# Score and maximum products of an attention kernel on halves of the array, two heads side by side

## Chip, cores and metric

One Trainium2 chip; the program runs on one of its cores. The metric is the time of one execution on the device, in microseconds. PE is the matmul engine (PEld its weight loads), DVE the vector engine, ACT the scalar engine, POOL the general one (GpSimd), SP the engine that issues most DMAs.

## What is computed

One transformer block on x of [4, 2048, 256] in fp32: causal attention with 16 heads of 16 dimensions, then a mixture of 16 experts (4 chosen per token) and one shared expert, each with its layer norm and modulation.

```python
h = layernorm(x) * (1 + ca) + sa
q, k, v = split(h @ qkv_w + qkv_b)             # [b, 16 heads, 2048, 16]
q, k = rotary(q), rotary(k)
scores = q @ k.T * 16 ** -0.5                  # causal mask
x = x + ga * ((softmax(scores) @ v) @ out_w + out_b)
h = layernorm(x) * (1 + cb) + sb
tidx, tw = route(h)                            # 4 of 16 experts
x = x + gb * (sum_e combine_e * w2_e(silu(w1_e h) * (w3_e h)) + shared(h))
```

## The kernel before

`plan()` writes one list of work items by hand; each engine walks the list in the same order and issues its part of each item, with semaphore waits between engines. So the list alone sets the order on all engines and on the queues of SP and POOL.

**qkv stage.** 16 chunks of 512 tokens. Rotated q and k are split into three bf16 parts each (high, middle, low: k = 0, 1, 2), stored to memory as `qk_parts`. The maxima of head group 0 are computed in between (`early`, `fill`), in PSUM banks 1 and 7 in turn.

**Attention.** A group is four heads of one batch; 16 groups (g), each with 40 steps (i) of 128 keys by up to 512 queries. Parts are loaded into `QO` and `KO` (three sets, in turn) by items `loadg`, 9 loads a group (L719), laid out along the partitions so that one product of 96 rows adds up six part products: q0k0, q1k0, q2k0, q0k1, q1k1, q0k2. Two more rows, 96 and 97, hold the negated row maximum in two bf16 parts on the query side (POOL's DMA, L1599) and ones on the key side.

- `max` (L930 to L933): for the group to come, queries in 128 rows against up to 512 keys; on the diagonal a second product (identb by m1, 128 rows) adds the mask. DVE reduces each bank (L1334), 160 a group. The banks are 4, 5 and 6 in turn (`Units`); a product waits until the reduction of three before it is done. `neg` and `nturn` (L939, L1347, L1349) turn the maxima of one head into a row.
- `st` (L952): four scores a step, 98 rows, one head each, into banks 0 to 3; `exp` (ACT, L1502) takes two banks at a time. POOL cuts the diagonal (L1619).
- `pv` (L971): four value products in fp32, each on its own 32 columns of the array, two steps behind.
- projection, norm and router logits of a finished batch (`project`, L983, L993, L1004), routing of the first half (`route`, on DVE) and its scatter (`scatter`, POOL's indirect DMAs, L1669) are pumped in, so many slots a step.

Between the four scores of a step stand single maxima: st, max, st, exp, max, pv, max, st, max, st, exp.

**Expert stage.** 143 + 143 jobs of 128 slots and 64 jobs of the shared expert, a pipeline of four items (`jin` L1022, `jgate` L1033, `jturn` L1046, `jdown` L1060). In the first 143 jobs the rest of the last batch's projection, the routing of the second half and its scatter are pumped at 2.65 slots a job: one list, one rate. SP loads the rows to scatter (L801), the rows of the jobs (L819), and stores the results (L833), all in one queue.

## Time and profile before

| | |
|---|---|
| runs | 3535.3, 3529.62, 3533.96 us; median 3533.96 |
| profiled execution | 3538.17 us, its span 3536.4 us |
| granted PE clock, mean | 0.949 |
| busy PE / DVE / ACT / POOL | 3129.2 / 2286.6 / 1608.0 / 1313.5 us |
| attention, first to last exponential | 347.7 to 2326.4 us |
| head groups 1, 2, 5, 6 | 106.8 us each |
| groups with projection (3, 4, 7, 8, 11, 12) | 128 to 143 us |
| groups 9, 10, 13, 14, 15 | 120.0, 117.3, 139.3, 119.4, 92.7 us |
| expert stage | from 2328 us to the end |

A group ends with its fourth copy of the outputs (L1509). A record of PE shows the time until the result is modelled to be there, so records overlap; how long PE is held is read from one start to the next.

### The profile page before, as it was taken

How to read it: one execution, taken by the hardware profiler on the slowest of the kernel's cores; microseconds unless marked ns; L12 is line 12 of the kernel's file. 1: busy time of each engine (PE TensorE's matmuls, PEld its weight loads, DVE VectorE, ACT ScalarE, POOL GpSimd, SP SyncE). 2: the span in 40 equal slices, each digit the busy share in tenths (PEclk: the TensorE clock that was granted, in tenths of full speed). 3: DMA queues.
4: the chain of work that ended last, by engine and by line, in shares of the span. 5: the costliest groups of instructions: out<-in, count | busy, mean ns of one | idle time of the engine just before them, and what ended most of it. 6: DMA issues, size and time to landing. Idle time of an engine off the chain costs nothing.

```text
span 3536.4 us, 50303 instructions
## 1 busy us (share of the span) xinstructions
PE 3129.2 (88%) x17106; PEld 1518.3 (43%) x17108; DVE 2286.6 (65%) x4981; ACT 1608.0 (45%) x2593; POOL 1313.5 (37%) x1684
## 2 busy tenths in 40 slices
PE   8776799999999999999998888989986779999778
PEld 4433233344333344233343222346654446666555
DVE  8887588887788877999877767224631124443466
ACT  3322466655566654566554555733322223333222
POOL 6755111234212244211265555331025543331453
PEclk9998899999999999999999989989997889999899
DMA  5733521232122213212234432343344445553565
GB/s 171 196 94 109 89 51 31 46 79 71 39 56 51 54 52 79 47 29 47 62 109 105 104 90 77 116 111 95 96 130 148 152 136 148 146 148 114 151 181 154
DMA packets 280103, 350.21 MB, mean 99 GB/s; under 512 B 58968, under 2 KB 236776, under 8 KB 279592
## 3 DMA queue, kind: packets, MB, share of 16 engines
q1 hardware_dynamic: 248972, 271.79, 29.5%
q0 software_dynamic: 30208, 71.87, 6.9%
q10 hardware_dynamic: 672, 3.34, 0.4%
q8 instruction: 141, 2.31, 0.3%
q14 instruction: 110, 0.90, 0.1%
HBM read 206.51 MB, written 139.21 MB: 98 GB/s over the span
## 4 chain that ended last, share of the span: by engine, by line
PE 67%; DVE 16%; issue 6%; another core or an unknown queue 4%; DMA 2%; POOL 2%; ACT 2%; SPq 1%; DVEq 0%; POOLq 0%; ACTq 0%
PE PB L930 13%; PE PB L1033 13%; PE PB L971 12%; DVE mx L1334 10%; PE PB L952 9%; PE PB L1060 8%; PE PB L983 3%; PE PB L1046 2%; PE PB L1022 2%; PE PB L933 1%; PE PB L901 1%; DMA KO<-qk_parts 1%; DVE xn L1287 1%; PE PB L912 1%
## 5 line engine op out<-in xcount | busy, mean ns | idle before, releaser
L1334 DVE TENSOR_REDUCE mx<-PB 128x1 f32<-128x512 f32 (+3 forms) x2560 | 1409.0, 602 | 289.5 <-PE PB L933 149.3
L1502 ACT ACTIVATE P<-PB 128x1024 f32<-128x1024 f32 (+3 forms) x1280 | 1102.3, 895 | 812.7 <-PE PB L952 759.1
L930 PE MATMUL PB<-KO,QO 96*128 96x512 bf16 (+3 forms) x2560 | 901.0, 357 | 105.9 <-DVE mx L1334 67.8
L952 PE MATMUL PB<-QO,KO 98*128 98x512 bf16 (+3 forms) x2560 | 824.2, 353 | 16.0 <-DVE PB L1359 11.6
L971 PE MATMUL PB<-P,V 128*17 128x512 f32 (+3 forms) x5120 | 605.3, 545 | 17.0 <-POOL P L1619 16.7
L930 PEld LDWEIGHTS PB<-KO,QO 96*128 96x128 bf16 x2560 | 251.0, 98 | 789.7 <-DVE mx L1334 517.4
L1033 PE MATMUL PB<-W,xT 128*128 (+1 forms) x1400 | 554.3, 521 | 40.0 <-issue 32.7
L1426 DVE TENSOR_TENSOR ha<-sl,PB 128x192 f32<-128x192 f32 x350 | 123.7, 353 | 535.4 <-ACT sl L1547 406.7
L1060 PE MATMUL PB<-W,haT 96*128 (+1 forms) x1400 | 381.6, 396 | 62.1 <-issue 34.0
L1619 POOL TENSOR_SCALAR_AFFINE_SELECT P<-P 128x256 f32<-128x256 f32 x512 | 207.4, 414 | 582.7 <-ACT P L1502 578.0
L1682 POOL DMA_INDIRECT yg<-y_slots,sidu x256 | 244.0, 953 | 396.4 <-DVE acc L1418 191.9
L952 PEld LDWEIGHTS PB<-QO,KO 98*128 98x128 bf16 x2560 | 243.6, 100 | 247.2 <-ACT P L1502 91.5
L1033 PEld LDWEIGHTS PB<-W,xT 128*128 128x128 f32 x1400 | 253.9, 202 | 160.0 <-issue 75.1
L1554 ACT ACTIVATE haT<-PB 96x256 f32<-96x256 f32 x350 | 132.7, 379 | 388.2 <-PE PB L1046 259.5
L1547 ACT ACTIVATE sl<-PB 128x192 f32<-128x192 f32 x350 | 115.5, 330 | 403.6 <-PE PB L1033 281.7
L1060 PEld LDWEIGHTS PB<-W,haT 96*128 96x128 f32 x1400 | 248.2, 197 | 94.4 <-issue 57.4
L933 PE MATMUL PB<-m,identb 128*128 128x128 bf16 x1024 | 229.4, 224 | 0.0
L1669 POOL DMA_INDIRECT x_slots<-Rsg,sidu x172 | 166.8, 970 | 89.3 <-issue 44.4
L1434 DVE COPY yo<-PB 128x256 f32<-128x256 f32 x286 | 120.6, 422 | 115.7 <-PE PB L1060 49.9
L1046 PE MATMUL PB<-ident,ha 128*96 128x128 f32 x700 | 142.2, 285 | 57.0 <-DVE ha L1426 38.7
L1599 POOL DMA_DIRECT2D QO<-nh x128 | 66.7, 523 | 307.6 <-DVE nh L1349 305.8
L971 PEld LDWEIGHTS PB<-P,V 128*17 128x17 f32 x5120 | 85.8, 95 | 201.1 <-issue 165.0
(157 smaller groups left out, 2821.8 us busy)
## 6 DMA issues: line engine op xcount, KB each, us to landing
xq<-x_slots SPq DMA_DIRECT2D x286, 128.0 KB
y_slots<-yo SPq DMA_DIRECT2D x286, 128.0 KB
qk_parts<-pt SPq DMA_DIRECT2D x192, 128.0 KB, 2.4
KO<-qk_parts SPq DMA_DIRECT2D x96, 256.0 KB, 5.3
rden<-rden_rows SPq DMA_DIRECT2D x256, 64.0 KB
QO<-qk_parts SPq DMA_DIRECT2D x16, 768.0 KB, 7.9
v_rows<-vst SPq DMA_DIRECT2D x16, 544.0 KB, 3.4
V<-v_rows SPq DMA_DIRECT2D x16, 544.0 KB, 5.9
```

What stands on the lines that cost most here:

```text
L930: mm = pe.matmul(PB[:, bank, 0:n], QO[0:96, k3, j, 128 * t:128 * t + 128], KO[0:96, k3, j, 512 * kc:512 * kc + n], start=True, stop=True)
L933: mm = pe.matmul(PB[:, bank, n - 128:n], identb[:, :], m1[:, :], start=False, stop=True, skip_group_check=True)
L952: mm = pe.matmul(PB[:, j, 0:n], KO[0:98, k3, j, 128 * kt:128 * kt + 128], QO[0:98, k3, j, q0:q0 + n], start=True, stop=True)
L971: mm = pe.matmul(PB[32 * j:32 * j + 17, 7, c0:512], V[:, g % 2, kt, 17 * j:17 * j + 17], P[:, pbuf(g, i, j // 2), j % 2, 0:n], start=kt == ...
L1033: mm = pe.matmul(PB[:, 2 + k, 0:2 * I], xT[:, k, f, :], W13[f][:, expert(n), :], start=f == 0, stop=f == 1)
L1046: mm = pe.transpose(PB[0:IH, 4 + k, 128 * f:128 * f + 128], ha[:, k, IH * f:IH * f + IH], ident[:, :])
L1060: mm = pe.matmul(PB[:, bank, 0:256], haT[:, k, f, :], W2[f][:, expert(n), :], start=f == 0, stop=f == 1)
L1334: dve.tensor_reduce(mx[:, j, t, kc:kc + 1], PB[:, u.bank[item], 0:n], AX.X, ALU.max).then_inc(s["mx"], 1)
L1502: act.activation(P[:, pbuf(g, i, p), :, 0:n], PB[:, 2 * p:2 * p + 2, 0:n], ACT.Exp, scale=0.25).then_inc(s["exp"], 1)
L1619: pool.affine_select(out=P[:, k, :, 0:128], in_=P[:, k, :, 0:128], compare_op=ALU.is_ge, fill=0.0, base=0, pattern=[[0, 2], [1, 128]], cha ...
L1669: pool.indirect_dma_start(xg_d[p][:, :], bass.IndirectOffsetOnAxis(sidu[:, i, j:j + 1], 0), hs[k], None).then_inc(s[f"w_s{p}{k}"], 16)
L1682: pool.indirect_dma_start(yg[:, k, j, :], None, y_d[p][:, :], bass.IndirectOffsetOnAxis(sidu[:, i, j:j + 1], 0)).then_inc(s[f"l_yg{k}"], 16)
```

## The change

- **Layout.** Each head uses 98 of 128 partitions in two parts. For an even head of the group, rows 0 to 63 hold four part products (q0k0, q1k0, q0k1, q1k1), rows 64 to 95 the other two (q2k0, q0k2), rows 96 and 97 the maximum. For an odd head the halves are swapped: 64 to 127, 0 to 31, 32 and 33. The loads are 20 a group (`LOADS`), each for two heads, one a step instead of one every third step.
- **Maxima.** A product of 64 rows over four part products. `max_items` gives the heads of a pair in turn, so neighbours stand in different halves of the array; their `neg` and `nturn` come after both. The mask is two products of 64 rows, of 128 and 64 columns (`pick`, `tri`).
- **Scores.** `st` issues two heads' first passes (64 rows) side by side; `st2` waits for both (semaphore `sa`) and adds two second passes (34 rows) in the other half of the array, into the same banks. Maxima stand between `st` and `st2`.
- **Pumps in the first 143 jobs.** Projection and routing at 4 slots a job; the scatter, once the routing is done, at 1.8.
- `tile_e0` and `tile_e1` share one tile, at partitions 0 and 32.

```diff
+LOADS = [(z, 64 * odd + row, odd, k, n) for odd in (0, 1)
+         for z, row, k, n in ((0, 0, 0, 2), (0, 32, 0, 2), (1, 0, 0, 1), (1, 16, 0, 1), (1, 32, 1, 1), (1, 48, 1, 1))]
+LOADS += [(z, 64 - 64 * odd + row, odd, k, 1) for odd in (0, 1) for z, row, k in ((0, 0, 2), (0, 16, 0), (1, 0, 0), (1, 16, 2))]
+NL = len(LOADS)
...
-    for j in range(4):
+    for j in (0, 2):
         for t in range(16):
             for kc in range(t // 4 + 1):
                 yield ("max", g, j, t, kc)
-        yield ("neg", g, j)
-        yield ("nturn", g, j)
+                yield ("max", g, j + 1, t, kc)
+        for k in (j, j + 1):
+            yield ("neg", g, k)
+            yield ("nturn", g, k)
...
             o("st", g, i, 0)
-            one()
-            o("st", g, i, 1)
+            maxima((done + want + 2) // 4 * 2)
+            o("st2", g, i, 0)
             o("exp", g, i, 0)
-            one()
             if len(pend) == 2:
                 values(*pend.pop(0))
-            one()
-            o("st", g, i, 2)
-            one()
-            o("st", g, i, 3)
+            o("st", g, i, 1)
+            maxima(want)
+            o("st2", g, i, 1)
             o("exp", g, i, 1)
...
-            if g < 14 and 0 <= part < 27 and part % 3 == 0:
-                o("loadg", g + 2, part // 3)
+            if g < 14 and 0 <= part < NL:
+                o("loadg", g + 2, part)
...
-    run(0, NI[0], (chain(proj[3], route(1), scatter(1)), 2.65))
+    run(0, NI[0], (chain(proj[3], route(1)), 4), (chain(once("route", 1, ROUTE_SLOTS - 1), scatter(1)), 1.8))
...
-                    mm = pe.matmul(PB[:, bank, 0:n], QO[0:96, k3, j, 128 * t:128 * t + 128], KO[0:96, k3, j, 512 * kc:512 * kc + n],
+                    half = slice(64 * (j % 2), 64 * (j % 2) + 64)
+                    mm = pe.matmul(PB[:, bank, 0:n], QO[half, k3, j, 128 * t:128 * t + 128], KO[half, k3, j, 512 * kc:512 * kc + n],
                                    start=True, stop=True)
                     if kc == t // 4:
-                        mm = pe.matmul(PB[:, bank, n - 128:n], identb[:, :], m1[:, :], start=False, stop=True, skip_group_check=True)
+                        pe.matmul(PB[:, bank, n - 128:n], pick[half, 0, :], tri[half, 0, :], start=False, stop=True, skip_group_check=True)
+                        mm = pe.matmul(PB[:, bank, n - 64:n], pick[half, 1, :], tri[half, 1, 64:128], start=False, stop=True,
+                                       skip_group_check=True)
...
+                    for j in (2 * p, 2 * p + 1):
+                        rows = slice(64 * (j % 2), 64 * (j % 2) + 64)
+                        pe.matmul(PB[:, j, 0:n], KO[rows, k3, j, 128 * kt:128 * kt + 128], QO[rows, k3, j, q0:q0 + n],
+                                  start=True, stop=False).then_inc(s["sa"], 1)
+                elif name == "st2":
...
+                    q.wait_ge(s["sa"], 2 * o.n(*item))
+                    for j in (2 * p, 2 * p + 1):
+                        rows = slice(64 - 64 * (j % 2), 98 - 64 * (j % 2))
+                        mm = pe.matmul(PB[:, j, 0:n], KO[rows, k3, j, 128 * kt:128 * kt + 128], QO[rows, k3, j, q0:q0 + n],
+                                       start=False, stop=True)
+                    mm.then_inc(s["st"], 1)
```

**Where it moves instructions.** The order on PE in group 5, between the value products of steps 19 and 20 (counted from 0), before (maxima L930, mask L933, scores L952, values L971):

```order
L930 MATMUL PB<-KO,QO 128x512
L933 MATMUL PB<-m_51,identb 128x128
L952 MATMUL PB<-QO,KO 128x384
L930 MATMUL PB<-KO,QO 128x512
L952 MATMUL PB<-QO,KO 128x384
L930 MATMUL PB<-KO,QO 128x512
L952 MATMUL PB<-QO,KO 128x256
L930 MATMUL PB<-KO,QO 128x128
L933 MATMUL PB<-m_51,identb 128x128
L952 MATMUL PB<-QO,KO 128x256
L930 MATMUL PB<-KO,QO 128x512
L971 MATMUL PB<-P,V 17x512 x4
```

The same place in the changed kernel (maxima L941, masks L944 and L945, first passes L968, second passes L979, values L997):

```order
L968 MATMUL PB<-QO,KO 128x384 x2
L941 MATMUL PB<-KO,QO 128x512 x2
L979 MATMUL PB<-QO,KO 128x384 x2
L968 MATMUL PB<-QO,KO 128x256 x2
L941 MATMUL PB<-KO,QO 128x256
L944 MATMUL PB<-tri,pick 128x128
L945 MATMUL PB<-tri,pick 128x64
L941 MATMUL PB<-KO,QO 128x256
L944 MATMUL PB<-tri,pick 128x128
L945 MATMUL PB<-tri,pick 128x64
L979 MATMUL PB<-QO,KO 128x256 x2
L997 MATMUL PB<-P,V 17x512 x4
```

Scores come in pairs with maxima between the passes. Over all groups 1060 of 1280 second passes have a maximum ahead of them since their first pass; the 220 others are 22 in group 0, 80 in group 15, and 118 in the rest. Diagonal maxima of a pair stand three products apart.

The order on PE in the qkv stage (qk L901, v L912 and group 0's maxima), before:

```order
L901 MATMUL PB<-hT,wqk_s 128x512
L930 MATMUL PB<-KO,QO 128x128
L933 MATMUL PB<-m_51,identb 128x128
L901 MATMUL PB<-hT,wqk_s 128x512
L930 MATMUL PB<-KO,QO 128x256
L933 MATMUL PB<-m_51,identb 128x128
```

and changed (qk L911, v L922):

```order
L911 MATMUL PB<-hT,wqk_s 128x512
L941 MATMUL PB<-KO,QO 128x256
L944 MATMUL PB<-tri,pick 128x128
L945 MATMUL PB<-tri,pick 128x64
L911 MATMUL PB<-hT,wqk_s 128x512
L941 MATMUL PB<-KO,QO 128x512 x2
L922 MATMUL PB<-wv_s,hT 128x256 x2
```

The fp32 products of the qkv stage and the bf16 products alternate as before. What differs is that the bf16 ones now take halves of the array: passing from an undivided product to one in row halves or back occurs 184 times here and 353 times in attention, where before both used the whole array.

The order on SP in the expert stage while POOL scatters (L801 loads rows for the scatter), before:

```order
L801 DMA Rsg<-h_rows 128x256
L833 DMA y_slots<-yo 128x256
L819 DMA xq_146<-x_slots 128x256
L801 DMA Rrk<-h_rows 128x256
L833 DMA y_slots<-yo 128x256
L819 DMA xq_146<-x_slots 128x256
L833 DMA y_slots<-yo 128x256
L819 DMA xq<-x_slots 128x256
L801 DMA Rsg<-h_rows 128x256
L833 DMA y_slots<-yo 128x256
```

and changed (L811 is the same load, L843 the store, L829 the jobs' load):

```order
L811 DMA Rrk<-h_rows 128x256
L843 DMA y_slots<-yo 128x256
L829 DMA xq<-x_slots 128x256
L843 DMA y_slots<-yo 128x256
L829 DMA xq<-x_slots 128x256
L811 DMA Rsg<-h_rows 128x256
L843 DMA y_slots<-yo 128x256
L829 DMA xq<-x_slots 128x256
L843 DMA y_slots<-yo 128x256
L829 DMA xq_145<-x_slots 128x256
L843 DMA y_slots<-yo 128x256
```

A load for the scatter stands after every one or two jobs before, after every two or three in the changed kernel; the scatter goes from job 56 to 136 instead of from 86 to 140.

## Rows read from the trace of the kernel before

**Rows 1.** Busy time by stretch: groups 1, 9, 13 and 15 of attention, whole engines.

```profile
core 0: us, PE busy (x) PEld busy (x) DVE busy (x) ACT busy (x) POOL busy (x), PEclk, DMA share, GB/s
494.90:601.70 106.80, 104.33 (x710) 36.43 (x708) 90.56 (x177) 69.56 (x86) 21.78 (x44) 1.00 0.24 47
...
1459.00:1579.00 120.00, 109.77 (x710) 35.72 (x708) 111.41 (x230) 70.12 (x86) 24.39 (x44) 0.99 0.21 41
...
1976.40:2115.80 139.40, 116.84 (x709) 37.61 (x708) 92.77 (x177) 70.85 (x86) 84.23 (x109) 0.89 0.42 111
...
2235.20:2327.90 92.70, 87.71 (x576) 32.85 (x576) 12.20 (x45) 69.14 (x89) 40.32 (x69) 1.00 0.39 124
```

**Rows 2.** Groups of instructions by shape in group 1: busy, mean ns, idle before.

```profile
L1334 DVE TENSOR_REDUCE mx<-PB 128x1 f32<-128x512 f32 x113 | 72.2, 682 | 5.9 <-PE PB L930 4.1 <-PE PB L933 0.9
...
L930 PE MATMUL PB<-KO,QO 96*128 96x512 bf16 x113 | 42.9, 382 | 0.5 <-DVE mx L1334 0.4
...
L971 PE MATMUL PB<-P,V 128*17 128x512 f32 x224 | 29.5, 598 | 0.0
```

**Rows 3.** Timeline of group 5: start us, us, engine line op, in order of time.

```profile
1001.50 0.38 PE L952 MATMUL PB<-QO,KO 98*128 98x512 bf16 x1
...
1001.92 1.02 ACT L1502 ACTIVATE P<-PB 128x1024 f32<-128x1024 f32 x1 [0.55 <-PE PB L952]
...
1006.38 0.38 PE L930 MATMUL PB<-KO,QO 96*128 96x512 bf16 x1
...
1006.69 1.05 PE L971 MATMUL PB<-P,V 128*17 128x512 f32 x8
...
1007.68 0.39 PE L930 MATMUL PB<-KO,QO 96*128 96x512 bf16 x1
...
1007.90 0.38 PE L952 MATMUL PB<-QO,KO 98*128 98x512 bf16 x1
...
1008.12 0.38 PE L930 MATMUL PB<-KO,QO 96*128 96x512 bf16 x1
...
1008.34 0.22 PE L933 MATMUL PB<-m,identb 128*128 128x128 bf16 x1
...
1008.40 0.38 PE L952 MATMUL PB<-QO,KO 98*128 98x512 bf16 x1
```

**Rows 4.** Timeline of DVE in group 10: reductions without a wait.

```profile
1590.13 2.47 DVE L1334 TENSOR_REDUCE mx<-PB 128x1 f32<-128x512 f32 x4
```

**Rows 5.** Waits in group 1: engine line <- waited for: us in total, times, longest.

```profile
PEld PB L930 <- DVE mx L1334: 29.9, 56, 0.9
```

**Rows 6.** Waits in group 15.

```profile
PEld PB L952 <- ACT P L1502: 29.2, 42, 0.9
```

**Rows 7.** Timeline of group 15: score products followed by a projection.

```profile
2265.80 0.60 PE L952 MATMUL PB<-QO,KO 98*128 98x512 bf16 x2
...
2266.24 1.89 PE L983 MATMUL PB<-wo_s,ON 128*128 128x256 f32 x8
```

**Rows 8.** Waits in the second half of the qkv stage.

```profile
PEld PB L930 <- DVE mx L1334: 55.8, 75, 3.8
```

**Rows 9.** SP's queue and PE's wait at the start of attention.

```profile
364.21 1.39 SPq L719 DMA_DIRECT2D QO<-qk_parts  x3
365.65 3.22 SPq L719 DMA_DIRECT2D KO<-qk_parts  x6
...
PEld PB L930 <- DMA KO<-qk_parts: 21.9, 1, 21.9
```

**Rows 10.** Expert stage by stretch: L1060 alone, then L1022 alone.

```profile
2450.00:2500.00 50.00, 19.11 (x74) 12.21 (x72) 1.00 0.32 95
...
3000.00:3100.00 100.00, 37.65 (x147) 25.11 (x148) 1.00 0.50 145
...
2613.00:2880.00 267.00, 23.89 (x112) 17.82 (x112) 0.83 0.46 149
```

**Rows 11.** Waits of SP's queue, ACT and POOL in time, while scatters run.

```profile
SPq L833 <- DVE yo L1434: 118.4, 27, 12.9
...
2712.43 0.38 ACT L1554 ACTIVATE haT<-PB 96x256 f32<-96x256 f32 x1 [6.73 <-remote]
...
2708.00 0.96 POOL L1669 DMA_INDIRECT x_slots<-Rrk,sidu  x1 [0.30 <-issue]
2709.27 0.96 POOL L1669 DMA_INDIRECT x_slots<-Rrk,sidu  x1 [0.30 <-issue]
```

More of the change, by code:

```diff
@@ L182, in plan @@
         if c == 5:
-            for part in range(9):
+            for part in range(NL):
                 o("loadg", 0, part)
@@ L268, in plan @@
     proj = [project(b) for b in range(4)]
-    for part in range(9):
+    for part in range(NL):
         o("loadg", 1, part)
@@ L370, in run, with once @@
             drain(f[0])
-    run(0, NI[0], (chain(proj[3], route(1), scatter(1)), 2.65))
+    def once(name, *at):
+        while not o.has(name, *at):
+            yield
+    run(0, NI[0], (chain(proj[3], route(1)), 4), (chain(once("route", 1, ROUTE_SLOTS - 1), scatter(1)), 1.8))
     o("second")
@@ L857, in expert @@
                     half = i // RB % 2 * RB
-                    pe.load(pe_regs[half:half + k], tile_e[p][0:1, i:i + k])
+                    pe.load(pe_regs[half:half + k], tile_e[p][:, i:i + k])
                     for j in range(k):
```

77 lines of the change are left out of this document (43 added, 34 removed).

## Prediction

> **What bounds the kernel now.** I read the busy time of each stretch first, because the profile's 88% for PE is an average over stages with different limits. Attention runs 16 head groups of 40 steps. A group without projection work, such as group 1, takes 106.8 us; there PE is busy 104.3 us, DVE 90.6 and ACT 69.6 [rows 1]. In group 9 the routing joins and DVE reaches 111.4 of 120.0. In group 13 POOL scatters. Group 15 has no maxima left, and DVE falls to 12.2 of 92.7. Next the groups of instructions inside group 1: DVE stood idle only 5.9 us before the 113 widest reductions, PE 0.5 us before the widest maxima [rows 2]. So both are near their limits, and PE is the tighter one.
>
> PE's records are longer than what they occupy, so I read starts. In group 5 a 512-column bf16 product is followed by the next start after 0.22 us, though its record says 0.38; a 128-column one after 0.06 [rows 3]. The value product (L971, eight records side by side) starts 0.31 us after the product ahead of it, 0.09 more than 0.22, and holds the array 0.99 us, where four streams of 0.22 would need 0.86: 0.13 more. The mean product is 435 columns wide (24 full steps and 16 averaging 320), 0.185 us. Group 1 then needs 320 products x 0.185 = 59.2, 64 masks x 0.06 = 3.8, 40 value products x (0.09 + 0.13 + 0.74) = 38.4, in all 101.4 us of its 106.8; the rest is mostly four turns of the maxima, before which PE waits for DVE. DVE needs 0.60 us for a 512-column reduction: four take 2.47 us, of which the last record is 0.68 [rows 4]. An off-diagonal maximum therefore gives PE 0.22 plus its share of the step's other work, (59.2/2 + 38.4)/160 = 0.43, together 0.65, against DVE's 0.60. That is the parity which limits what a faster PE can bring.
>
> **The maxima.** Each head now contracts 64 rows in its own half of the array, and two heads stand side by side. Off the diagonal there are 96 products in a group (24 per head), 48 pairs; if the halves overlap, a pair costs 0.22 instead of 0.44, so 48 x 0.22 = -10.6 us per group. No row shows two row halves at once. The nearest is L971: eight records with a mean of 598 ns lie in 0.99 us [rows 2, 3], four column strips side by side. Bounds: no overlap, 0 gained; full overlap, -10.6. I take full overlap, since L971 is the same array divided the other way. On the diagonal the order puts three products of one head before three of the other, so only the last 64 columns meet the partner: no gain there. The split mask is a second instruction, 0 to 0.06 us; 64 x 0.04 = +2.6 us.
>
> **The scores.** Four products a step become eight, in four pairs. With overlap the streaming is equal; four steps of 128 columns gain 4 x 4 x 0.056 = +0.9 us, because they are issue-bound. Without overlap it would be 160 x 0.185 = +29.6 us per group. The second pass waits for the semaphore of the first. A record of 0.38 us against a start distance of 0.22 leaves 0.16 us, and about 0.04 for the signal (ACT starts 0.04 us after such a record's end, 1001.92 against 1001.88), 0.2 us in all [rows 3]. What covers it is one pair of maxima (0.22). The order has 1060 of 1280 second passes with at least one maximum ahead. The 118 without that lie outside group 15 and group 0's start are 8 a group x 0.2 = +1.6; those with a single narrow one +0.6; the weight load that is no longer fetched early, 80 x 0.02 (bounds 0 and 0.10, its record) = +1.6. Behind that wait on PE stand the second pass, the value product and the next maxima; ACT's exponential waits for the second pass, and DVE, when it catches up, for the maxima.
>
> Per group: -10.6 + 2.6 + 0.9 + 1.6 + 0.6 + 1.6 = -3.3 us. DVE's floor of about 90 us allows it, but a pair needs two of three banks free at once. PE already waited 29.9 us before weight loads of maxima for DVE in group 1 [rows 5], mostly hidden under the product ahead. I keep -3.3 in groups 1 to 7 (-23) and half in groups 8 to 14 (-12), where DVE or the scatters end more waits. Groups 0 (11 steps) and 15 (40) have no maxima: 102 waits x 0.2 = +20, of which I take +14, because PE waits 29.2 us for ACT in group 15 anyway and may hide some [rows 6]. Maxima and scores together: **-21 us**.
>
> **Changes of the array's division.** Before, maxima, scores, projection, turns and qkv all used the undivided array, and PE passed between them without a gap: two score products start at 2265.80 and the projection 0.44 us later, just 2 x 0.22 [rows 7]. Only the value product divides it, and pays 0.09 going in and 0.13 coming out. Now every bf16 product is in row halves, so each meeting with an undivided fp32 product is a new change: counted from the order, 353 in attention and 184 in the qkv stage. Bounds: 0 (the 0.22 belongs to L971's column strips or to fp32 alone) and 0.11 each, 39 + 20 = +59 us. I take **+24 us**, under half: in the qkv stage PE waits for DVE before the maxima as it is (55.8 us over 75 waits [rows 8]), which covers some. The Trainium skill (TensorEngine Tiling (Array Packing), Key Properties) says that changing the tiling mode drains the engine. By that rule all 537 changes would cost; the trace agrees with it for the value product [rows 3], and no run here shows it for row halves.
>
> **Loads and small work.** A group's parts come in 20 loads instead of 9, with the same bytes; from group 2 on one a step, a group ahead of their readers, where SP has time. One place is exposed: group 1's loads are issued in a burst, from 364.21 on, nine in 4.6 us, and PE then waits 21.9 us for them before the first maximum [rows 9]. Twenty issues at 0.5 us put the last one 5.5 us later. Bounds: 0 (bytes decide) and +5.5; I take **+3 us**. The same burst for group 0 lies in the qkv stage beside other work, and behind it SP's stores of parts have time to spare: 0, with +5.5 if they have not. POOL's rows of negated maxima keep number and size; the DVE setup instructions added lie ahead of the first chunk, about 1 us.
>
> **The expert stage.** The pumps are changed too. The last projection and routing go at 4 slots a job, the scatter at 1.8 instead of 2.65. In the order the scatter began at job 86 and ended at 140; now it runs from 56 to 136. Before it a job (four L1060 records, 18.4 jobs in 50 us) takes 2.7 us; during it two L1022 records a job make 56 jobs in 267 us, 4.8 each [rows 10]. SP waits 118.4 us there for DVE's output copies, not for the scatters, and ACT once sits 6.73 us before work that is ready, put down to "remote" [rows 11]. So the scatters slow 54 jobs by 2.1 us each, 113 us, or 0.8 us per POOL instruction (145). If that price is per scatter, thinning them brings nothing: 0. If the scatters' time is their own (255 us for 145, whatever the jobs do), 80 jobs fit where 54 did: 26 x 2.7 = -70 us. The gathers later, one per job of 2.7 us, show no such price, which speaks for one that falls with density. I take **-25 us**, nearer the first end, because 1.8 times POOL's spacing of 1.26 us [rows 11] is still 2.27 of a 2.7 us job. That case would be wrong on the other side if every job during scatters is slowed: 26 more jobs at up to 2.1 us, +55.
>
> **Sum.** -21 + 24 + 3 - 25 = -19 us on the profiled execution's 3538.17: 3519. The median of the runs shown is 3533.96, 4 us lower, so **3515 us**, 0.5% below it. About 0.2%, 7 us, is what can be told from no change.
>
> **Rivals.**
> 1. *The changes of division are dear*: PE empties the array at all 537. The rule of the Trainium skill named above (TensorEngine Tiling (Array Packing), Key Properties) would have it so. The sum is -21 + 59 + 3 - 25 = +16, 3534 + 16 = 3550 us, slower. It decides from 43 us on, 0.08 us each, if the tail gives 25. For: the 0.22 us around every L971. Against: PE has slack in the qkv stage. Chance 0.22.
> 2. *The halves overlap badly.* With half the overlap, scores cost +15 and maxima save 5 less: +17 us in each of 15 groups, 3534 + 255 = 3790; with none, 29.6 x 16 over 4000. Against: L971's strips. For: no row shows row halves. Chance 0.08.
> 3. *Better than forecast.* PE's relief pays in full, -7 a group to DVE's floor (-100), the tail gives -60, and changes of division cost nothing: 3534 - 100 + 14 - 60 = 3390; half of it, 3450, is more likely. Chance 0.22.
> 4. *DVE keeps the pace*: bursts of two maxima into three banks leave it as late as before, attention gains nothing and the scatters keep their price: 3534 + 14, then 0 to 24 more: 3548 to 3572. Chance 0.13.
>
> My forecast keeps 0.35, spread over 3495 to 3540. Cases 1, 2 and 4 and a part of mine are slower: 0.38; within 0.2%: 0.14; faster: 0.48. The range reaches to 3430 (case 3 in part) and 3610 (case 1 with case 4), leaving out case 2 and the far end of case 3.
>
> **What would show it.** Right: two maxima of neighbouring heads start within 0.06 us, and a pair is followed after 0.22; second passes start about 0.43 us after the first; group 1 takes 103 to 105 us; group 15 100 to 107; scatter jobs fall from 4.7 us to about 4. A gap of 0.1 us before a projection that follows a score shows case 1. Pairs 0.4 us apart show case 2. Group 1 unchanged with DVE idle under 5 us shows case 4. The forecast is wrong if attention, from 347.7 to 2327.9 before, changes by over 60 us either way.

## The result, and the profile after

Four executions of the changed kernel took 3696.03 to 3703.71 us, median 3701.64; four of the kernel before on the same chip 3529.62 to 3535.3, median 3534.32. The ratio is 1.0475, 95% interval 1.0458 to 1.0491: slower by 4.7%. The forecast was 3515 us, range 3430 to 3610. It was wrong in sign and out of its range.

The profiled execution of the changed kernel has a span of 3702.0 us, 165.6 more than before. I cut both spans at the same places (a group ends with its fourth copy of the outputs):

| stretch, us | before | after | difference | forecast |
|---|---|---|---|---|
| up to the first exponential (qkv stage) | 347.7 | 358.2 | +10.5 | part of +24 |
| group 0 | 147.2 | 162.4 | +15.2 | about +3, and loads +3 |
| groups 1, 2, 5, 6 | 106.8 each | 115.8 each | +9.0 each | -3.3 each |
| groups 3, 4, 7 | 128.5, 137.2, 128.5 | 140.0, 144.8, 139.9 | +30.5 | -9.9 and part of +24 |
| groups 8 to 14 | 919.0 | 1008.2 | +89.2 | -12 and part of +24 |
| group 15 | 92.7 | 111.1 | +18.4 | about +11 |
| the rest (expert stage) | 1208.6 | 1174.2 | -34.4 | -25 |

The busy time by stretch in the changed kernel, for groups 0, 1, 9, 13 and 15 in this order; the last four answer to [rows 1]:

```profile
358.20:520.60 162.40, 135.86 (x969) 37.93 (x967) 92.42 (x183) 75.07 (x86) 21.43 (x45) 0.83 0.35 65
520.60:636.40 115.80, 106.84 (x935) 33.14 (x934) 89.84 (x177) 72.29 (x85) 21.84 (x44) 1.00 0.20 43
...
1562.60:1695.00 132.40, 119.11 (x934) 35.42 (x934) 111.01 (x230) 72.94 (x85) 23.86 (x44) 0.91 0.18 38
...
2127.40:2286.90 159.50, 119.74 (x933) 34.72 (x932) 90.95 (x177) 72.93 (x85) 82.77 (x106) 0.87 0.34 96
2416.70:2527.80 111.10, 103.84 (x731) 35.40 (x732) 12.19 (x45) 69.94 (x88) 40.34 (x69) 1.00 0.32 105
```

In group 1 the clock is fully granted, DVE works as long as before (89.84 against 90.56), and both engines idle more: DVE 26.0 us instead of 16.2. No engine got a new amount of work that fills the 9 us; most of it is waiting. The groups of instructions by shape in group 1, which answer to [rows 2]:

```profile
L1365 DVE TENSOR_REDUCE mx<-PB 128x1 f32<-128x512 f32 x113 | 71.0, 683 | 15.3 <-PE PB L941 14.2 <-PE PB L945 1.0
...
L941 PE MATMUL PB<-KO,QO 64*128 64x512 bf16 x113 | 31.9, 379 | 3.9 <-DVE mx L1365 2.3
```

DVE stood idle 15.3 us before the widest reductions, 5.9 before the change: it now waits for PE's maxima. And PE's waits in the same group, beside [rows 5]:

```profile
PEld PB L941 <- DVE mx L1365: 20.2, 48, 0.7
...
DVE mx L1365 <- PE PB L941: 14.2, 24, 1.0
...
DVE mx L1365 <- PE PB L945: 8.3, 8, 3.8
PEld PB L979 <- PE PB L968: 9.0, 29, 0.4
```

So PE and DVE wait for each other in turn, and PE waits for itself (the second pass for the first). The sum of the weight loads' waits for DVE is no measure of the loss: it was 29.9 us before and is 20.2 now, and much of it lies under products that still run. The timeline of PE's products in group 5 shows how; columns are start us, us, engine, line and operation:

```profile
1067.55 0.39 PE L968 MATMUL PB<-QO,KO 64*128 64x512 bf16 x2
1067.77 0.38 PE L941 MATMUL PB<-KO,QO 64*128 64x512 bf16 x2
1068.03 0.39 PE L979 MATMUL PB<-QO,KO 34*128 34x512 bf16 x2
1068.25 0.38 PE L968 MATMUL PB<-QO,KO 64*128 64x512 bf16 x2
1068.47 0.84 PE L941 MATMUL PB<-KO,QO 64*128 64x512 bf16 x2
1068.94 0.60 PE L979 MATMUL PB<-QO,KO 34*128 34x512 bf16 x2
```

The halves do overlap. Two products of 512 columns stand in one record of 0.39 us, and the next pair starts 0.22 us later: each pair costs what one product did. But the second pair of maxima (1068.47) finds one bank free where it needs two, and its second product waits for DVE. DVE and PE's weight loads at the same place:

```profile
1068.18 1.89 DVE L1365 TENSOR_REDUCE mx<-PB 128x1 f32<-128x512 f32 x3 [0.72 <-PE PB L941]
...
1068.93 0.09 PEld L941 LDWEIGHTS PB<-KO,QO 64*128 64x128 bf16 x1 [0.58 <-DVE mx L1365]
```

DVE had idled 0.72 us until the first pair came (1068.18). 0.29 us later the second pair begins, and its second product waits until 1068.93. Two pairs, 0.7 us apart, want four banks and there are three; then value products pass in which DVE gets nothing new. No run gave the maxima a fourth bank.

The second loss is plain in group 15, which has no maxima. Its timeline, beside [rows 7]:

```profile
2480.28 0.39 PE L979 MATMUL PB<-QO,KO 34*128 34x512 bf16 x2
2480.60 0.62 PE L1030 MATMUL PB<-gw_s,lT 128*128 128x16 f32 x4
2481.07 0.41 PE L1019 MATMUL PB<-ident,h2t 128*128 128x128 f32 x2
2481.42 0.39 PE L968 MATMUL PB<-QO,KO 64*128 64x512 bf16 x2
2481.90 0.39 PE L979 MATMUL PB<-QO,KO 34*128 34x512 bf16 x2
2482.22 1.05 PE L997 MATMUL PB<-P,V 128*17 128x512 f32 x8
2483.20 0.39 PE L968 MATMUL PB<-QO,KO 64*128 64x512 bf16 x2
2483.68 0.39 PE L979 MATMUL PB<-QO,KO 34*128 34x512 bf16 x2
```

The second passes start 0.48 us after the first (2483.20, 2483.68), where the 512 columns would allow 0.22: 0.26 uncovered, twice a step, 80 times in the group, an estimate of 20.8 us. The waits of group 15 put it down by name; the second line answers to [rows 6]:

```profile
PEld PB L979 <- PE PB L968: 29.9, 77, 0.6
PEld PB L968 <- ACT P L1533: 18.6, 26, 0.9
```

The third loss is in the same timeline: from a pair in halves to an undivided product it takes 0.32 us (2480.28, 2480.60), not 0.22.

A fourth part of the loss stands in the clock column of the rows. TensorE's clock was granted at one of two levels, 2.4 or 1.2 GHz, and a mean below 1.00 stands for time at the lower one, which counts as one half. Group 0 has 0.83; before, the same group had 0.90:

```profile
347.70:494.90 147.20, 119.59 (x728) 35.91 (x727) 92.12 (x182) 74.41 (x87) 21.46 (x45) 0.90 0.41 71
```

Group 9 has 0.91 and had 0.99 [rows 1]. From PE's timeline in group 9, with the clock at its lower level from about 1639.0 to 1649.2:

```profile
1636.85 0.85 PE L941 MATMUL PB<-KO,QO 64*128 64x512 bf16 x2 [1.09 <-DVE mx L1365]
...
1647.34 1.91 PE L997 MATMUL PB<-P,V 128*17 128x512 f32 x8
1649.18 0.41 PE L968 MATMUL PB<-QO,KO 64*128 64x512 bf16 x2
```

PE had waited 1.09 us for DVE shortly before the clock fell, and the value product then holds the array 1.84 us instead of 0.98 (2482.22 to 2483.20). What a stretch loses to the clock is therefore at most its length times what its mean lacks of 1.00. By this estimate group 0 lost 27.6 us against 14.7 before, group 9 11.9 against 1.2, and the whole span 3702.0 x 0.063 = 233 against 3536.4 x 0.051 = 180. So up to some 53 of the 165.6 us are time at the lower clock: 8 of the +10.5 in the qkv stage, 13 of the +15.2 in group 0, about 48 of the +89.2 in groups 8 to 14, about 5 in groups 3, 4 and 7, none in groups 1, 2, 5, 6 and 15; and about 20 of the 34.4 us that the expert stage gained. Whether PE's new waits brought the lower clock or only stand beside it, no run here parts.

### The profile page after: what moved, and what is told of

Same layout as the page of the kernel before. It is cut to its first block, busy times and chain, and to the rows that moved or that the text cites. A ratio compares the mean times of both kernels' runs of the same rounds, so it can differ in the third digit from the quotient of the medians.

```text
span 3702.0 us, 57660 instructions
## 1 busy us (share of the span) xinstructions
PE 3237.6 (87%) x20690; PEld 1482.0 (40%) x20692; DVE 2273.4 (61%) x4990; ACT 1638.6 (44%) x2593; POOL 1314.9 (36%) x1685
## 4 chain that ended last, share of the span: by engine, by line
PE 40%; DVE 9%; another core or an unknown queue 5%; issue 3%; ACT 1%; POOL 1%; DMA 1%; SPq 0%; DVEq 0%; POOLq 0%; ACTq 0%
PE PB L1059 12%; PE PB L1086 7%; DVE mx L1365 6%; PE PB L997 6%; PE PB L968 3%; PE PB L941 3%; PE PB L979 3%; PE PB L1072 2%; PE PB L1048 2%; PE PB L1009 2%; ACT sl L1578 0%; ACT P L1533 0%; PE PB L1030 0%; ACT xT L1569 0%
## 5 line engine op out<-in xcount | busy, mean ns | idle before, releaser
L1533 ACT ACTIVATE P<-PB 128x1024 f32<-128x1024 f32 (+3 forms) x1280 | 1135.0, 896 | 967.9 <-PE PB L979 908.8
L941 PE MATMUL PB<-KO,QO 64*128 64x512 bf16 (+3 forms) x2560 | 684.3, 360 | 146.3 <-DVE mx L1365 99.2
L979 PE MATMUL PB<-QO,KO 34*128 34x512 bf16 (+3 forms) x2560 | 598.6, 366 | 53.6 <-remote 35.6
L997 PE MATMUL PB<-P,V 128*17 128x512 f32 (+3 forms) x5120 | 624.9, 561 | 4.0 <-POOL P L1652 3.9
L968 PE MATMUL PB<-QO,KO 64*128 64x512 bf16 (+3 forms) x2560 | 498.4, 366 | 13.6 <-DVE PB L1390 12.1
L941 PEld LDWEIGHTS PB<-KO,QO 64*128 64x128 bf16 x2560 | 198.4, 96 | 478.2 <-DVE mx L1365 372.6
L968 PEld LDWEIGHTS PB<-QO,KO 64*128 64x128 bf16 x2560 | 137.7, 95 | 552.2 <-issue 287.9
L1578 ACT ACTIVATE sl<-PB 128x192 f32<-128x192 f32 x350 | 115.5, 330 | 378.7 <-PE PB L1059 269.6
L979 PEld LDWEIGHTS PB<-QO,KO 34*128 34x128 bf16 x2560 | 154.4, 94 | 228.7 <-PE PB L968 172.6
L1702 POOL DMA_INDIRECT x_slots<-Rsg,sidu x172 | 166.6, 968 | 138.2 <-DMA Rsg<-h_rows 94.6
L1661 POOL TENSOR_TENSOR ON<-osb,rden 128x512 f32<-128x512 f32 x64 | 82.5, 1289 | 352.7 <-DMA rden<-rden_rows 266.5
L944 PE MATMUL PB<-tri,pick 64*128 64x128 bf16 x1024 | 193.5, 223 | 0.0
```

The lines of the kernel that those rows point to most:

```text
L941: mm = pe.matmul(PB[:, bank, 0:n], QO[half, k3, j, 128 * t:128 * t + 128], KO[half, k3, j, 512 * kc:512 * kc + n], start=True, stop=True)
L944: pe.matmul(PB[:, bank, n - 128:n], pick[half, 0, :], tri[half, 0, :], start=False, stop=True, skip_group_check=True)
L968: pe.matmul(PB[:, j, 0:n], KO[rows, k3, j, 128 * kt:128 * kt + 128], QO[rows, k3, j, q0:q0 + n], start=True, stop=False).then_inc(s["sa"], 1)
L979: mm = pe.matmul(PB[:, j, 0:n], KO[rows, k3, j, 128 * kt:128 * kt + 128], QO[rows, k3, j, q0:q0 + n], start=False, stop=True)
L997: mm = pe.matmul(PB[32 * j:32 * j + 17, 7, c0:512], V[:, g % 2, kt, 17 * j:17 * j + 17], P[:, pbuf(g, i, j // 2), j % 2, 0:n], start=kt == ...
L1533: act.activation(P[:, pbuf(g, i, p), :, 0:n], PB[:, 2 * p:2 * p + 2, 0:n], ACT.Exp, scale=0.25).then_inc(s["exp"], 1)
```

## The experiments

The chips differ. On one the kernel before took about 3357 us (e1 to e6), on the others 3526 to 3543. The same kernel was profiled on a quick chip and on a slow one as e1 and e15: groups 12 to 14 and the expert stage, in which POOL scatters or gathers, hold the whole difference (1408.7 and 1585.5 us), and group 1 takes 106.8 us on both, as the changed kernel's takes 115.8 wherever it was profiled. So times are compared as ratios to the kernel before on the same chip, and groups by their own length.

### The pumps, alone and undone

`e1` is the kernel before with the new pumps, `e2` the changed kernel with the old ones.

```diff
-    run(0, NI[0], (chain(proj[3], route(1), scatter(1)), 2.65))
+    run(0, NI[0], (chain(proj[3], route(1)), 4), (chain(once("route", 1, ROUTE_SLOTS - 1), scatter(1)), 1.8))
```

> The kernel before with the changed pumps alone: projection and routing at 4 slots a job, the scatter at 1.8. Theory A (thinned scatters slow the jobs less, whatever attention does): the expert stage, 1209 us before and 1174 in the changed kernel, takes 1174, so 3500 us. Rival (the stage gained only because of what attention left it with): 3534 us.

> The changed kernel with the pumps of before (one list at 2.65). Theory A: the expert stage goes back to 1209 us, 3702 + 35 = 3737 us, attention as it was. Rival: 3702 us.

Measured: e1 3339.1 us, ratio 0.9948 (0.9931 to 0.9964); e2 3532.19 us, 1.0521 (1.0503 to 1.0539). The pumps gain 19 us on this chip; what is slower is all in the halves. On the chip of the first result the stretch after attention shrank by 34.4 us, and the windows show where. Columns here are those of [rows 10]; the scatters' stretch of before, then of after (PE's L1022 and L1048, two records a job):

```profile
2646.60:2866.00 219.40, 20.07 (x92) 14.85 (x92) 0.82 0.46 149
```

```profile
2776.80:3023.00 246.20, 28.67 (x144) 21.41 (x144) 0.92 0.50 161
```

46 jobs at 4.77 us became 72 at 3.42, with 128 scatters in either stretch. The price of a job does fall with the scatters' density. Part of the fall is the clock's (0.82 and 0.92): without at most 0.86 and 0.27 us a job, by the estimate above, 3.91 and 3.15 are left.

### Bursts and the wait of the second pass

`e4` issues the maxima one at a time again, one between the passes of each pair of heads, one on either side of the value product, and what is left at the step's end:

```diff
-            maxima((done + want + 2) // 4 * 2)
+            one()
             o("st2", g, i, 0)
             o("exp", g, i, 0)
+            one()
             if len(pend) == 2:
                 values(*pend.pop(0))
+            one()
             o("st", g, i, 1)
-            maxima(want)
+            one()
             o("st2", g, i, 1)
             o("exp", g, i, 1)
+            while done < want:
+                one()
```

> The changed kernel with its maxima placed one at a time (one between the passes, one on either side of the value product, one between the passes) in place of two bursts. Theory B (bursts of two into three banks leave holes of 1.7 us in which DVE runs dry, then PE waits for banks): group 1 falls from 115.8 us to 108 to 110, 3702 - 80 = 3620 us. Theory C (what costs is the wait of the second pass, which one maximum covers about as well as two, and pairs that no longer stand together add up to 10.6 us a group): group 1 stays or grows, 3702 to 3800 us.

`e5` lets the second pass read rows of the half in which the first ran, and so needs no wait. It leaves two part products and the row maximum out, and it moves the pass to the other half as it drops the wait; no run parts these two, and "the wait" below stands for both:

```diff
-                    q.wait_ge(s["sa"], 2 * o.n(*item))
...
-                        rows = slice(64 - 64 * (j % 2), 98 - 64 * (j % 2))
+                        rows = slice(64 * (j % 2), 64 * (j % 2) + 34)
```

> The changed kernel with the second pass in the same half of the array as the first and so with no wait between them; it adds 34 rows of the first half in place of the two part products and the maximum, so the scores are others. Group 15 has a second pass 0.48 us behind the first, 0.22 of it streaming: 80 x 0.26 = 21 us. Theory C: group 15 falls from 111 to 92 us and group 1 by 6 us or more, 3702 - 110 = 3590 us. Theory B: group 15 falls as much, but group 1 by 2 us at most, 3702 - 50 = 3650 us.

`e7` is both, and `e9` the changed kernel once more, beside it. All of e3, e4, e5 and e7 hold the new pumps, so a ratio below 1 is not the halves' gain by itself.

> Spread maxima (as in the run before) and the second pass in the same half without a wait (it adds 34 rows of the first half, so the scores are others). Group 1 was 115.8 with bursts, 115.1 with bursts and no wait, 110.0 spread. If the wait costs only where nothing covers it: group 1 at 108.5 to 110, group 15 at 94.7. If the bursts hid the wait's price: group 1 at 106.8 or below.

> The changed kernel once more, beside the kernel before on the chip of these runs. The kernel with the old pumps was at 3532 us beside 3358, and the pumps alone took 19 us off the kernel before: so 3515 us, a ratio of 1.047 as in the first comparison. Group 1 at 115.8 us.

| | ratio (interval) | group 1 | group 15 |
|---|---|---|---|
| changed kernel (e9) | 1.0476 (1.0448 to 1.0504) | 115.8 | 111.0 |
| e4, no bursts | 1.0297 (1.0266 to 1.0328) | 110.0 | 111.1 |
| e5, no wait | 1.0366 (1.0349 to 1.0383) | 115.1 | 94.7 |
| e7, neither | 0.9942 (0.9919 to 0.9964) | 103.1 | 95.4 |

In group 1 the wait alone is worth 0.7 us and the bursts alone 5.8, but both together 12.7: while one is there, it stands in for much of the other. All of group 1's rows have a clock of 1.00, so none of this is the clock's. Group 15 splits them: without maxima only the wait counts, 16.4 us of its +18.4. In e4, with the bursts gone, the wait for the first pass comes forward; its row in group 1, where the changed kernel has 9.0:

```profile
PEld PB L983 <- PE PB L972: 22.9, 64, 0.6
```

The same spacing takes group 0 from 162.4 to 147.6 us with all 20 loads left as they are, so its +15.2 came with the bursts and not with the loads. Its clock rose with it, from 0.83 to 0.86, which is up to 7 of the 14.8 us.

### Whether the pairs pay

`e3` takes the heads' maxima in turn again, so that no two neighbours are in different halves:

```diff
-    for j in (0, 2):
+    for j in range(4):
         for t in range(16):
             for kc in range(t // 4 + 1):
                 yield ("max", g, j, t, kc)
-                yield ("max", g, j + 1, t, kc)
...
+        yield ("neg", g, j)
+        yield ("nturn", g, j)
```

> The changed kernel with the maxima of one head after the other, as before, so neighbours stand in the same half and cannot overlap each other. If overlap is worth what the forecast took, PE loses up to 10.6 us a group: group 1 from 115.8 to 122 to 126 us, 3702 + 110 = 3810 us. If the overlap is hidden under waits for DVE and for the second pass: group 1 within 2 us, 3702 +- 30 us.

Measured: 3538.0 us, 1.0534 (1.0505 to 1.0563), against 1.0521 (1.0503 to 1.0539) for e2 and 1.0476 (1.0448 to 1.0504) for the whole change on another chip. Group 1 takes 116.1 us against 115.8. The overlap of the maxima, forecast at 10.6 us a group, is worth 0.3 in this order; what the whole program shows of it lies in groups 0 (176.6 us, 163.9 in e2) and 8 (161.2, 150.5), and there the clock fell from 0.83 to 0.76 and from 0.92 to 0.86, by the estimate 15 and 11 us, as much as the difference. `e10` (changed) and `e11` (before) ask whether DVE hides it: DVE reduces half the columns only.

```diff
-                    dve.tensor_reduce(mx[:, j, t, kc:kc + 1], PB[:, u.bank[item], 0:n], AX.X, ALU.max).then_inc(s["mx"], 1)
+                    dve.tensor_reduce(mx[:, j, t, kc:kc + 1], PB[:, u.bank[item], 0:n // 2], AX.X, ALU.max).then_inc(s["mx"], 1)
```

> The changed kernel with DVE reducing only the first half of each tile of scores (it leaves the other half out of the maxima). Theory B (PE has room, the pace of DVE through three banks takes it back): group 1 falls from 115.8 us to 102 or less, below the 106.8 of the kernel before, since PE's need was put at 103.5. If PE itself is the longer one now: group 1 stays above 110 us.

> The kernel before with the same halved reductions. PE's need there was worked out at 101.4 us and the turns: group 1 falls from 106.8 to 102 to 104 us. If DVE held it as much as it holds the changed kernel: below 98 us.

Measured: e10 3477.98 us, 0.9837 (0.9811 to 0.9863), group 1 102.8 us; e11 3411.17 us, 0.9648 (0.9611 to 0.9685), group 1 103.8. The busy time of group 1 in e10, then in e11 (DVE's busy time stands behind PE's and PEld's):

```profile
479.40:582.20 102.80, 100.90 (x935) 32.92 (x934) 55.01 (x176) 70.76 (x86) 21.88 (x44) 1.00 0.23 49
```

```profile
459.40:563.20 103.80, 102.76 (x709) 36.53 (x708) 63.29 (x177) 69.48 (x86) 21.77 (x44) 1.00 0.26 48
```

With DVE out of the way the changed order needs 1.0 us less of PE than the old one, and with DVE at work 9.0 more: waits on DVE cost it 13.0 us and the kernel before 3.0. These 10.0 more and 1.0 less are the +9.0.

### The changes of division

`e6` is the kernel before with maxima of 64 rows, two of six part products left out, in one half of the array, beside masks, scores and projection of 96 to 128 rows. In group 1 the array's division then changes 336 times instead of 80, by the order of instructions.

```diff
-                    mm = pe.matmul(PB[:, bank, 0:n], QO[0:96, k3, j, 128 * t:128 * t + 128], KO[0:96, k3, j, 512 * kc:512 * kc + n],
+                    mm = pe.matmul(PB[:, bank, 0:n], QO[0:64, k3, j, 128 * t:128 * t + 128], KO[0:64, k3, j, 512 * kc:512 * kc + n],
```

> The kernel before with its maxima over rows 0 to 63 in place of 0 to 95 (it leaves two of the six part products out of the maxima), everything else and the order unchanged: undivided scores and masks alternate with products in a row half. Theory D (each change of the array's division costs 0.1 us, as the gaps of 0.09 and 0.10 around a projection in the changed kernel show): about ten changes a step more, 40 us a group on PE's path, group 1 from 106.8 to 140 us, 3534 + 500 = 4030 us. Rival (a product of 64 rows is no change by itself, the gaps come from the fp32 type): 3534 us.

Measured: 3833.38 us, 1.1426 (1.1361 to 1.149); group 1 130.1 us. 23.3 us more over 256 changes are 0.091 each (0.103 if e11's 103.8 is taken for PE's need before), and the timeline of PE in group 1 shows them one by one:

```profile
603.12 0.23 PE L933 MATMUL PB<-m,identb 128*128 128x128 bf16 x1
603.19 0.38 PE L952 MATMUL PB<-QO,KO 98*128 98x512 bf16 x1
603.50 0.39 PE L930 MATMUL PB<-KO,QO 64*128 64x512 bf16 x1
603.82 0.23 PE L933 MATMUL PB<-m,identb 128*128 128x128 bf16 x1
603.89 0.38 PE L952 MATMUL PB<-QO,KO 98*128 98x512 bf16 x1
```

From 603.19 to 603.50 is 0.31 us for 512 columns (undivided to half), from 603.50 to 603.82 is 0.32 (half to undivided), where 0.22 passes without a change; mask to score, both undivided, takes 0.07 (603.12, 603.19), against 0.06 in the kernel before [rows 3].

### The value product between the passes

`e8` gives the second pass of the second pair another cover, e4's value product, which takes 1 us:

```diff
+            o("st", g, i, 1)
             one()
             if len(pend) == 2:
                 values(*pend.pop(0))
             one()
-            o("st", g, i, 1)
-            one()
             o("st2", g, i, 1)
             o("exp", g, i, 1)
+            one()
```

> Spread maxima, and the value product moved between the two passes of the second pair, so that it covers one of a step's two waits. In group 15, where nothing else covers them, 40 of 80 waits of 0.26 us go: 111.1 to 101 us; in group 1, where single maxima covered most of a wait, 110.0 to 108.5. Whole 3457 - 35 = 3422 us beside a kernel before of 3357. If ACT's later exponential holds the banks instead: no gain, 3457 us.

Measured: 3694.09 us, 1.0473 (1.0443 to 1.0502), group 1 117.6 us against e4's 110.0, and group 15, for which 101 was expected, 115.5 against 111.1 (at most 3.5 of it at a lower clock, 0.97). A miss. In group 1 the wait for the first pass shrank as meant, but PE now waits for ACT to free the scores' banks (18.8 us, 3.4 in e4) and for DVE (34.6, 27.8 in e4). In group 15 the waits for the first pass even grew, from 29.6 us in e4 to 43.9. PE's weight loads in group 1:

```profile
PEld PB L945 <- DVE mx L1369: 34.6, 57, 0.9
PEld PB L972 <- ACT P L1537: 18.8, 34, 0.8
...
PEld PB L983 <- PE PB L972: 5.5, 14, 0.9
```

The first pass of the second pair now stands ahead of the value product, earlier than ACT has read its banks; the wait was moved in group 1, not covered. Why it grew in group 15 stays open.

### Both passes in a head's own half

`e12` keeps all part products and needs no wait: the second pass's operands of a head lie in that head's half, in the tile's column of its neighbour (`j ^ 1`); the two heads of a pair swap the places of these operands. The loads' column and POOL's rows of negated maxima move with them. On e4:

```diff
-LOADS += [(z, 64 - 64 * odd + row, odd, k, 1) for odd in (0, 1) for z, row, k in ((0, 0, 2), (0, 16, 0), (1, 0, 0), (1, 16, 2))]
+LOADS += [(z, 64 * odd + row, odd, k, 1) for odd in (0, 1) for z, row, k in ((0, 0, 2), (0, 16, 0), (1, 0, 0), (1, 16, 2))]
...
-                    q.wait_ge(s["sa"], 2 * o.n(*item))
...
-                        rows = slice(64 - 64 * (j % 2), 98 - 64 * (j % 2))
-                        mm = pe.matmul(PB[:, j, 0:n], KO[rows, k3, j, 128 * kt:128 * kt + 128], QO[rows, k3, j, q0:q0 + n],
+                        rows, sl2 = slice(64 * (j % 2), 64 * (j % 2) + 34), j ^ 1
+                        mm = pe.matmul(PB[:, j, 0:n], KO[rows, k3, sl2, 128 * kt:128 * kt + 128], QO[rows, k3, sl2, q0:q0 + n],
```

> Spread maxima, and each head's second pass in its own half: its two part products and its maximum rows lie in the neighbour's column slot of the same half, so all six part products and the maximum are there and no wait stands between the passes. Theory E (burst and wait each cost only where the other does not hide it; without both PE keeps a small gain): group 1 at 103.1 us as in the run that left parts out, group 15 at 95, ratio 0.994 to the kernel before. Rival (that run was quicker for another reason, its operands or loads): group 1 above 108 us, ratio 1.02.

`e13` is e12 with two maxima at a time again, one pair ahead of the value product and one behind it; `e14` is e12 with half the columns reduced (the edit of e10). The diff is that of e13.

```diff
-            one()
...
-            one()
+            upto = (done + want + 2) // 4 * 2
+            while done < min(upto, want):
+                one()
...
-            one()
+            while done < (want if want == len(mu) else want // 2 * 2):
+                one()
...
-            one()
...
-            while done < want:
-                one()
```

> The same layout, with both passes of a pair of heads back to back and the maxima in bursts of two before and after the value product, 1.1 to 1.3 us apart instead of 0.9 and 1.7. If even bursts let the pairs overlap and keep DVE fed: group 1 at 97 to 101 us, ratio 0.97. If any burst of two into three banks starves DVE: group 1 at 106 us or more, ratio 1.01.

> The own-half kernel with spread maxima and DVE reducing only the first half of each tile (it leaves the other half out of the maxima). This shows PE's own need in this order. The kernel before had 103.8 us this way, the changed one 102.8. With no wait, and maxima partly beside their neighbours: 96 to 99 us. If it stays at 102 or more, the side-by-side maxima are worth nothing even to PE.

Measured: e12 3515.21 us, 0.993 (0.9909 to 0.9952), group 1 103.1 us; e13 3552.81 us, 1.0037 (1.0019 to 1.0056), group 1 104.1; e14 3312.09 us, 0.9365 (0.9331 to 0.9399), group 1 93.2. e12 came out as expected; e13's 104.1 lies between its two theories and decides for neither; e14's 93.2 is below the 96 to 99 expected. Group 15 of e12 shows both passes of both pairs without a gap:

```profile
2254.68 1.05 PE L1001 MATMUL PB<-P,V 128*17 128x512 f32 x8
2255.66 0.39 PE L973 MATMUL PB<-QO,KO 64*128 64x512 bf16 x2
2255.89 0.38 PE L983 MATMUL PB<-QO,KO 34*128 34x512 bf16 x2
2256.11 0.38 PE L973 MATMUL PB<-QO,KO 64*128 64x512 bf16 x2
2256.33 0.38 PE L983 MATMUL PB<-QO,KO 34*128 34x512 bf16 x2
2256.64 1.05 PE L1001 MATMUL PB<-P,V 128*17 128x512 f32 x8
```

A step takes 1.96 us from value product to value product; in the changed kernel it took 2.48 (2482.22 to 2484.70). The busy time of group 1 in e12, and in e14, says what limits e12:

```profile
501.60:604.70 103.10, 99.69 (x937) 36.07 (x932) 89.30 (x177) 69.98 (x85) 21.70 (x44) 1.00 0.23 49
```

```profile
467.00:560.20 93.20, 92.20 (x938) 35.48 (x932) 56.74 (x176) 69.33 (x85) 21.62 (x44) 1.00 0.26 54
```

With DVE relieved PE alone needs 93.2 us where the kernel before needs 103.8 (e11): 10.6 less. That this is also the number forecast for the overlap of the maxima is a coincidence: in e14 single maxima and passes of different halves stand beside each other, split masks cost something, and no run takes the overlap of the maxima alone out of this order. With DVE at its full 89.3 us, 9.9 us of that are lost again to waits between the two.

e12 holds the new pumps too, so two kernels were run side by side for the share of each: `e15`, the kernel before with the new pumps (as e1), and `e16`, e12 unchanged.

> The kernel before with the new pumps of the first 143 jobs alone, once more, beside e16 on one chip. Theory P (the gain of the own-half version is the pumps' alone, its attention is only even with the kernel before): as much below the kernel before as e16 or more, 3500 to 3515 where the kernel before takes 3537 (the tail of the changed kernel took 34 us less than the tail before there), 3338 to 3343 where it takes 3357. Theory Q (the own-half attention gains by itself): e15 stays above e16 by more than 8 us.

> The own-half version (maxima one at a time, both passes of a head in its own half, new pumps), unchanged from e12. Theory P: its attention ends 5 to 20 us later than that of e15, since the changes of division in the qkv stage (some 9 us) and the groups with projection take back what groups 1, 2, 5 and 6 gain (3.7 us each), and its time is equal to that of e15 or up to 15 us longer. Theory Q: attention ends earlier than in e15, and the time is shorter by more than 8 us.

Measured: e15 3510.2 us, 0.9899 (0.9868 to 0.9931), attention's end at 2330.5 us; e16 3515.84 us, 0.993 (0.9905 to 0.9955), attention's end at 2330.8. The intervals overlap, and the ends of attention are equal, where theory P had expected e16's 5 to 20 us later: e16's first exponential comes 11.7 us later (358.0 against 346.3), groups 0 to 7 give back 26.5, 3.7 or 3.8 of it in each of the four without projection, and groups 8 to 15 take 15.1 of that again. Group 13 alone is 12.4 us longer there (150.6 against 138.2), with a clock of 0.83 against 0.90, by the estimate 12 us. What gains against the kernel before is the pumps. The best ratio of any kernel with all its work is that of e15, which has no halves at all; between it and the own-half version these runs tell no difference.

## Why the prediction was wrong, step by step

**The maxima overlap: mechanism right, value lost.** "I take full overlap, since L971 is the same array divided the other way" held: two products in 0.39 us, the next pair 0.22 us on. But in the changed order it bought 0.3 us a group instead of 10.6 (e3 against the change), and with DVE relieved the whole order gained PE only 1.0 us (e10, e11), not 3.3. PE's need of 101.4 us leaves out the four turns of the maxima, so e11's 103.8, which holds them, is near it. The +0.9 for narrow steps was wrong: in e12 two halves of 128 columns start together and the next pair 0.06 us later (2261.62, 2261.68), as one such product does.

**The step that failed: "Per group ... -3.3 us. DVE's floor of about 90 us allows it".** DVE's work allowed it; the order of arrivals did not. I wrote in the same place that a pair needs two of three banks free at once, and priced it at nothing in groups 1 to 7. It was worth the larger part of the +9.0: taking maxima one at a time gave back 5.8 us, and with the pass's wait gone too 12.7. Groups 1 to 7 came out at +66.5 us, not -23, groups 8 to 14 at +89.2, not -12 (about 48 of these at the lower clock). The parity of 0.65 and 0.60 us a maximum, which the prediction itself worked out, was the warning: with two engines that close, each burst made first one and then the other wait.

**The second pass's wait: undersized, and wrongly taken as covered.** Its uncovered price is 0.26 us, not 0.2 (0.48 from pass to pass, 0.43 expected). Group 15 took 111.1 us, over the 100 to 107 expected, and e5 gives 16.4 of its +18.4 back. I had taken less because PE waits for ACT there anyway. That hid little: those waits fell from 29.2 to 18.6 us, but 18.4 of the estimated 20.8 us came through. In groups with maxima I took one maximum as cover; e4's 64 waits of 22.9 us in group 1 show that the cover was thin, and e7 against e4 (103.1, 110.0) prices it at 6.9 us a group, with the bursts gone, where I had 2.2 (1.6 without cover, 0.6 with a narrow one).

**Changes of division: rival 1 was right as to the price.** 0.09 to 0.10 us each (e6: 23.3 us over 256), near the 0.11 end of my bounds, and the 0.32 us from L979 to L1030 is the gap of 0.1 that the prediction named as case 1's sign. The rule of the Trainium skill (TensorEngine Tiling (Array Packing), Key Properties) is that changing the tiling mode drains the engine. The traces agree with it for row halves too, by these 0.09 to 0.10 us at each change. In the qkv stage 184 changes at 0.09 would be 16.6 us; the stage grew by 10.5 (11.7 in e16 against e15), up to 8 of it at the lower clock, so 6 to 14 us were covered; that PE's waits for DVE covered them, as I had said, is likely and not shown. The loads of group 0 and the split masks are new in that stage as well; they weren't tried apart. For attention the record has a second price: groups 3 and 7 hold 42 such changes each in PE's trace, group 1 holds 8, and in e12, all at a clock of 1.00, groups 3 and 7 gain 0.3 us on the kernel before (128.2 against 128.5) where group 1 gains 3.7. That is 3.4 us for 34 more changes, 0.10 each, their full price, if nothing else differs between these groups. In the changed kernel group 3 loses 2.5 us more than group 1 (11.5 and 9.0), of which at most 1.4 at the lower clock. With 353 changes at 0.09 in attention and some 10 us in the qkv stage the term comes to about 42 us, an estimate, against the +24 taken.

**Loads: +3 was too much.** The twenty loads of group 1 do take 9.3 us of SP, from 375.28 on, but e4's group 0, with all of them, takes 147.6 us against 147.2 before. PE's weight loads wait 10.1 us for them in the changed kernel, less than the 21.9 of [rows 9].

**The clock: a term at nothing, without a reason.** The prediction has no line for it. The mean went from 0.949 to 0.937, at most some 53 us net, with +13 in group 0, about +48 in groups 8 to 14 and about -20 in the expert stage. That is a second thing that the sum had wrong beside the bursts, if it is one of its own and no consequence of them.

**The expert stage: right in sign, a little short.** -34.4 us against -25; about 20 of the 34.4 come with a higher clock (0.92 before, 0.94 after). On another chip e1 gained 19 us (3358.21 to 3339.1), and on a third e15 some 31 (medians 3541.27 and 3510.2). Jobs under scatters fell to 3.42 us, further than the "about 4". The jobs ahead of them, with 4 slots each, rose from 3.43 us (93 jobs in 318.7 us) to 3.95 (63 in 249.0), which took some of it back.

**The rivals.** Rival 2 (halves overlap badly) and rival 3 fell. Rival 4 had the right mechanism, bursts of two into three banks, and the wrong bound: it let bursts cost at most the gain and 24 us, "as late as before". It should have been let go beyond that, to what e10 and e11 show: waits on DVE of 13.0 us a group instead of 3.0. Its sign was wrong as well, "DVE idle under 5 us": DVE idled more, 15.3 before the widest reductions, because it was starved between bursts. With 10 us a group over 15 groups and rival 1's changes at 0.09 the sum is 3534 + 14 + 150 + 48 - 25 = 3721. That this lies near 3702 proves nothing: it is made after the result and has no term for the clock. In rival 3 the half way is 3461, not 3450, which changes nothing here.

## What to carry to other kernels

Where two engines take nearly the same time per item and few buffers stand between them, an edit that makes one faster but delivers in bursts can lose, as it did here; count buffers against the burst, and test by halving the consumer's work. Accumulating two passes in different halves of the array brought a semaphore wait here; laying both out in one half cost only addresses. Price every boundary between divided and undivided products, compare the granted clock stretch by stretch before a difference is put down to waits, and run a bundled edit's parts alone: here the part that gained had nothing to do with the halves.

## What the runs showed of the hardware

- Two products in the two row halves of the array ran side by side at no extra cost: 0.39 us for both with 512 columns, the next start after 0.22 to 0.23 us (1067.55, 1067.77).
- A change between undivided and row halves costs 0.09 to 0.10 us on PE, in either direction (0.091 over 256 changes in e6; 0.31 and 0.32 instead of 0.22 us at 512 columns).
- A second pass in the opposite half, ordered by a semaphore, started 0.48 us after the first; in the same half, without one, 0.23 us after it (2255.66, 2255.89).
- The time of a job under POOL's scatters depends on their density: 4.77 us with 128 scatters over 46 jobs, 3.42 over 72, against 2.7 without; the clock was 0.82, 0.92 and 1.00 there.
- At the lower clock a value product holds the array 1.84 us instead of 0.98.
- Two costs between PE and DVE, which run at nearly the same pace, did not add: 0.7 and 5.8 us alone, 12.7 together.
